# Second attention of a hybrid layer: scores, slot product and softmax two steps ahead of W2 instead of one

## The reference

```python
x = x + attn_a(layernorm(x))          # softmax attention, 16 heads of 128, (4, 256, 256) input
x = x + ffn(layernorm(x))             # int8-quantised 256x256 product
x = x + attn_b(layernorm(x))          # the attention of this document
x = x + ffn(layernorm(x))

def attn_b(hs):                       # per head: T = 256 positions, 128 features, M = 64 slots
    q, k = rope(hs @ Wq.T), rope(hs @ Wk.T);  v = hs @ Wv.T;  g = hs @ Wg.T
    s = clip(hs @ Ws1.T @ Ws2.T + bs2, -32, 32)
    es, enz = exp(s), exp(-cumlogsumexp(s, over positions))
    A  = tril(q @ k.T) * scale
    ok = enz * (A @ es);  qv = softmax(ok, over slots)
    W2 = tril((qv * enz) @ es.T)
    o  = W2 @ v
    o  = o * rsqrt(mean(o * o) + eps) * g_norm_weight * g * sigmoid(g)
    return o.reshape(T, H * 128) @ Wo.T
```

## Time and profile before

| | us |
|---|---|
| median of three runs (lowest, highest) | 821.48 (821.04, 825.55) |
| profiled execution, its own time | 821.59 |
| its span, first to last instruction | 819.7 |
| TensorE busy | 770.2 (94%) |
| VectorE busy | 581.3 (71%) |
| ScalarE busy | 435.4 (53%) |
| GpSimd busy | 285.7 (35%) |
| mean granted TensorE clock | 0.985 |

### The profile page before, as it was taken

How to read it: one execution, slowest core, us unless ns; L and a number is a source line. 1 busy time by engine, 2 the same in 40 slices (tenths; PEclk the granted TensorE clock), 3 DMA queues, 4 the chain that set the end, 5 groups by cost and what they waited for, 6 DMA issues and landing times.

```text
span 819.7 us, 14465 instructions
## 1 busy us (share of the span) xinstructions
PE 770.2 (94%) x4556; PEld 654.7 (80%) x4556; DVE 581.3 (71%) x1502; ACT 435.4 (53%) x1188; POOL 285.7 (35%) x291
## 2 busy tenths in 40 slices
PE   5899999999999995799999999999999999999963
PEld 4788888888888883478888888888888888888852
DVE  4555555555555558878887888798879888887686
ACT  3555565555556542465556465656564665555420
POOL 6311020201102014444536346355364463553222
PEclk9999999999999999899999999999999999999997
DMA  6110101101010100100101001001010010000001
...
DMA packets 23653, 23.74 MB, mean 29 GB/s; under 512 B 2369, under 2 KB 23361, under 8 KB 23506
## 3 DMA queue, kind: packets, MB, share of 16 engines
...
HBM read 22.45 MB, written 1.05 MB: 29 GB/s over the span
## 4 chain that ended last, share of the span: by engine, by line
PE 90%; DVE 5%; POOL 1%; ACT 1%; issue 1%; DMA 1%; SPq 0%; DVEq 0%; ACTq 0%; POOLq 0%
PE ps L1276 22%; PE ps L1483 11%; PE ps L1385 7%; PE ps L1283 5%; PE ps L1306 5%; PE ps L1349 3%; PE ps L1390 3%; PE ps L1495 3%; PE ps L1520 3%; PE ps L1325 3%; PE ps L1507 2%; PE ps L1402 2%; PE ps L1537 2%; PE ps L1539 2%; PE ps L1509 2%; PE ps L1508 2%
## 5 line engine op out<-in xcount | busy, mean ns | idle before, releaser
L1276 PE MATMUL ps<-xT_hi,w_hi 128*128 128x512 f32 x256 | 110.4, 431 | 5.3 <-DVE rot L1012 3.6
L1276 PE MATMUL ps<-xT_hi,w_lo 128*128 128x512 f32 x256 | 102.0, 399 | 0.0
L1276 PE MATMUL ps<-xT_lo,w_hi 128*128 128x512 f32 x256 | 101.5, 396 | 0.0
L1042 DVE TENSOR_TENSOR wt<-ps,const 128x384 f32<-128x384 f32 x128 | 68.2, 554 | 40.4 <-PE ps L1496 20.4
L383 POOL TENSOR_TENSOR w_lo<-w_raw,w_hi 128x512 fp32r<-128x512 f32 x32 | 40.8, 1285 | 155.8 <-ACT w_hi L535 154.1
L439 POOL TENSOR_TENSOR rot_s<-rot_s,const 128x512 f32<-128x512 f32 x64 | 82.1, 1293 | 21.1 <-ACT rot_s L678 21.1
L580 ACT ACTIVATE wt<-wt,negmax 128x128 f32<-128x128 f32 (+1 forms) x128 | 56.7, 444 | 28.2 <-DVE negmax L906 28.2
L894 DVE TENSOR_TENSOR v<-ps,bv_b 128x256 f32<-128x256 f32 x64 | 27.0, 422 | 51.9 <-PE ps L1283 51.9
L697 ACT ACTIVATE v<-ps 128x256 f32<-128x256 f32 x64 | 24.5, 382 | 72.4 <-PE ps L1483 72.2
L1276 PEld LDWEIGHTS ps<-xT_hi,w_hi 128*128 128x128 f32 x256 | 49.0, 192 | 15.1 <-issue 4.5
L1031 DVE RECIPROCAL enz<-zs 128x128 f32<-128x128 f32 x64 | 60.3, 943 | 1.0 <-ACT zs L684 1.0
...
## 6 DMA issues: line engine op xcount, KB each, us to landing
...
```

The lines of the kernel that those rows point to most:

```text
L1042: d.tensor_tensor(dst, src[:, 0:384], tri3, ALU.mult).then_inc(done, 1)
L1276: ins = mm(PJ[n[0]], w[:, m, c, h * P:(h + 1) * P], x[:, c, cols], start=(t == 0), stop=(t == len(terms) - 1))
```

## The change

One step more of lead, and everything is moved to fit:

- scores, slot scores, the exponential, its sum and the slot product are those of step x + 2 instead of x + 1; okeps has two halves, since two of them are now in use
- the transposes of qp and the copy zT are those of x + 1: they stand ahead of o, a whole step ahead of the W2 that reads them (`b_slot_transpose`, `b_z_copy`)
- projections move one step ahead: s to k1 stand in steps 1 and 3 of the step before, c0 to c3 in steps 0 and 2. `ti, tb` name the step that they used to stand in. So the prologue has the first s to k0 (k1 on TensorE) and the scores of step 1, and the last pair has projections in step 0 alone
- the order within a step is new on each engine; weight splits move from steps 1 and 2 to steps 0 and 1.

The core of the diff: the prologues of GpSimd and ScalarE, the new body and prologue of VectorE and TensorE. `...` marks what is left out; the lines taken out of a body stand in the functions above. ScalarE's and GpSimd's bodies change in the same manner.

```diff
@@ -506,6 +511,11 @@
...
+exp_tail(1, 1)
+rope_mul(slot_done(0, 1, B_TASKS.index("q0")), 0, 0)
+rope_mul(slot_done(0, 1, B_TASKS.index("q1")), 0, 1)
+rope_mul(slot_done(0, 1, B_TASKS.index("k0")), 1, 0)
+slots(1, 1)
...
@@ -794,8 +813,16 @@
...
+        s1_copy(3)
...
+b_task(0, 0, NB - 1, 0, 0)
+b_z_copy(0)
+b_task(0, 1, B_TASKS.index("s"), 1, 1)
+b_task(0, 1, B_TASKS.index("q0"), 1, 1)
+b_task(0, 1, B_TASKS.index("q1"), 1, 1)
+b_task(0, 1, B_TASKS.index("z"), 1, 1)
+b_task(0, 1, B_TASKS.index("k0"), 1, 1)
+b_okexp_step(1)
...
@@ -1068,100 +1095,105 @@
...
+def b_slots(x, k):
...
+    d.scalar_tensor_tensor(out=okeps[:, k, :], in0=oksum[:, :], scalar=RMS_EPS, in1=oksum[:, :],
...
+        ti, tb = (i, b + 1) if b < B - 1 else (i + 1, 0)
+        rest = not (last and b >= 1)
+        nxt = not (last and b >= 2)
+        half = 1 - tb // 2
+        phase = 2 * ti + 1 + tb // 2
...
+        def n(name):
+            j = B_TASKS.index(name)
+            return (*slot(ti, 1 + tb // 2, j), slot_ps(ti, 1 + tb // 2, j))
+        if b % 2 == 1:
+            if not (last and b == 3):
+                b_gate(slot(ti, tb // 2, NB - 1), phase - 1, 3, tb // 2)
+            if rest:
+                b_clip_s(n("s"), phase)
...
+            if last and b == 3:
+                ln_stats(3, 2, b_.y_acc, y_count(2))
+                ffn_out(1, 0)
+            if rest:
+                b_rope_cos(n("q0"), 0, 0)
+            if not (last and b == 3):
+                b_recip(None, tb // 2, 3)
+            if nxt:
+                b_scores(x + b + 2)
+            if rest:
+                b_rope_cos(n("q1"), 1, 0)
+            b_gated(x + b, b)
+            if rest:
+                b_recip(n("z"), half, 0)
+                b_rope_add(4 * phase + 1, 0, 0, half)
+            if nxt:
+                b_okn_max(x + b + 2, (b + 2) % B, 2 * i + (b + 2) // 2)
+            if not last:
+                out_tail(b_, x + b, b, O_)
+            if rest:
+                b_rope_cos(n("k0"), 0, 1)
+            if last and b == 3:
+                ffn_out(1, 1)
+                ln_scale(3, 2)
+                ffn_range(1, 2)
+            (add_y if last else add_group)(b_, x + b, b)
+            if rest:
+                b_rope_add(4 * phase + 2, 1, 0, half)
+            if nxt:
+                b_slots(x + b + 2, b % 2)
+        else:
+            if rest:
+                b_rope_add(4 * phase + 3, 0, 1, half)
+            for h in range(2):
+                b_mask(wt2[:, h, :], W_[h], b_w2_ps, 2 * (x + b) + h + 1, b_w2)
+            if rest:
+                b_rope_cos(n("k1"), 1, 1)
+                b_rope_add(4 * phase + 4, 1, 1, half)
...
+                b_gate(n("c0"), phase, 0, half)
+                b_recip(None, half, 1)
...
+                b_scores(x + b + 2)
+            b_gated(x + b, b)
+            if rest:
+                b_gate(n("c1"), phase, 1, half)
+                b_recip(None, half, 2)
+                b_gate(n("c2"), phase, 2, half)
+            if nxt:
+                b_okn_max(x + b + 2, (b + 2) % B, 2 * i + (b + 2) // 2)
...
+                b_slots(x + b + 2, b % 2)
...
+def n1(name):
+    j = B_TASKS.index(name)
+    return (*slot(0, 1, j), slot_ps(0, 1, j))
...
@@ -1198,8 +1230,20 @@
...
+b_slots(0, 0)
...
+b_gate(slot(0, 0, NB - 1), 0, 3, 0)
+b_clip_s(n1("s"), 1)
+b_rope_cos(n1("q0"), 0, 0)
+b_recip(None, 0, 3)
+b_scores(1)
+b_rope_cos(n1("q1"), 1, 0)
+b_recip(n1("z"), 1, 0)
+b_rope_add(5, 0, 0, 1)
+b_okn_max(1, 1, 0)
+b_rope_cos(n1("k0"), 0, 1)
+b_rope_add(6, 1, 0, 1)
+b_slots(1, 1)
...
@@ -1489,9 +1533,9 @@
...
-        if not (isinstance(x, int) and x == 0):
...
-            pe.wait_ge(b_w2, 2 * x + h - 1)
+        if not (isinstance(x, int) and x < 2):
...
+            pe.wait_ge(b_w2, 2 * x + h - 3)
...
@@ -1502,12 +1546,20 @@
...
+        pe.wait_ge(b_z, x)
...
+def b_slot_transpose(x):
...
+    pe.wait_ge(b_qp, x + 1)
+    for t in range(2):
+        ins = tr(X_qt[:, t * P:(t + 1) * P], qp[:, t, :], ident)
+    ins.then_inc(b_qt_ps, 1)
...
@@ -1543,72 +1595,34 @@
 def b_body(i, last):
     x = i * B
     for b in range(B):
...
+        ti, tb = (i, b + 1) if b < B - 1 else (i + 1, 0)
+        rest = not (last and b >= 1)
+        nxt = not (last and b >= 2)
+        half = 1 - tb // 2
+        phase = 2 * ti + 1 + tb // 2
+        c3_bank = slot(ti, 1 + tb // 2, NB - 1)[0]
+        if b % 2 == 1:
+            if rest:
+                b_task(ti, 1 + tb // 2, B_TASKS.index("s"), half, phase)
             b_w2_product(x, b, i)
...
             if last and b == 3:
                 ffn_product(1, 0)
                 ffn_transpose(1, 1)
+            if rest:
+                b_task(ti, 1 + tb // 2, B_TASKS.index("q0"), half, phase)
+            if not (last and b == B - 1):
+                b_slot_transpose(x + b + 1)
             b_o_product(x, b, i, last)
+            if rest:
+                b_task(ti, 1 + tb // 2, B_TASKS.index("q1"), half, phase)
             if nxt:
...
+                b_scores(x + b + 2, (b + 2) % B, 2 * i + (b + 2) // 2)
+            if rest:
+                b_task(ti, 1 + tb // 2, B_TASKS.index("z"), half, phase)
+                b_task(ti, 1 + tb // 2, B_TASKS.index("k0"), half, phase)
             if nxt:
...
+                b_ok(x + b + 2, (b + 2) % B, 2 * i + (b + 2) // 2)
             pe.wait_ge(b_og, x + b + 1)
             for h in range(2):
                 for t in range(2):
@@ -1618,9 +1632,7 @@
             if last and b == 3:
                 ffn_product(1, 1)
             if rest:
...
+                b_task(ti, 1 + tb // 2, B_TASKS.index("k1"), half, phase)
             if last:
                 pe.wait_ge(b_wos, PAIRS)
                 out_proj(b_, b, wos)
@@ -1628,7 +1640,44 @@
                 out_group(b_, i, b)
             if last and b == 3:
                 ffn_transpose(1, 2, (ffns[1].y, 1))
...
+        else:
+            b_w2_product(x, b, i)
+            if rest:
+                b_task(ti, 1 + tb // 2, B_TASKS.index("c0"), half, phase)
+            if last and b == 0:
+                out_group(b_, i, 0)
+            if rest:
+                b_task(ti, 1 + tb // 2, B_TASKS.index("c1"), half, phase)
+            if not (last and b == B - 1):
+                b_slot_transpose(x + b + 1)
+            b_o_product(x, b, i, last)
+            if nxt:
+                b_scores(x + b + 2, (b + 2) % B, 2 * i + (b + 2) // 2)
+            if rest:
+                b_task(ti, 1 + tb // 2, B_TASKS.index("c2"), half, phase)
+            if nxt:
+                b_ok(x + b + 2, (b + 2) % B, 2 * i + (b + 2) // 2)
+            pe.wait_ge(b_og, x + b + 1)
+            for h in range(2):
+                for t in range(2):
+                    o = (2 * h + t) * P
+                    ins = tr(O_[:, o:o + P], og[:, (2 * t + h) * P:(2 * t + h + 1) * P], ident)
+            ins.then_inc(b_ogt_ps, 1)
+            if rest:
+                b_task(ti, 1 + tb // 2, B_TASKS.index("et"), half, phase)
+            if last and b == 2:
+                for bank in range(2):
+                    pe.wait_ge(b_.proj_evac[bank], slot(PAIRS, 0, bank)[1])
+                ffn_transpose(1, 0)
+            if last:
+                pe.wait_ge(b_wos, PAIRS)
+                out_proj(b_, b, wos)
+            else:
+                out_group(b_, i, b)
+            if rest:
+                b_free(ti, 1 + tb // 2, NB - 1)
+                vg_chunk(c3_bank, 3, half, 0)
                 vg_chunk(c3_bank, 3, half, 1)
 pe.wait_ge(b_sums, 1)
@@ -1649,7 +1698,16 @@
         s1_product(2)
     if name == "et":
         s1_product(3)
+b_scores(1, 1, 0)
+b_slot_transpose(0)
+b_task(0, 1, B_TASKS.index("s"), 1, 1)
+b_task(0, 1, B_TASKS.index("q0"), 1, 1)
+b_task(0, 1, B_TASKS.index("q1"), 1, 1)
+b_ok(1, 1, 0)
+b_task(0, 1, B_TASKS.index("z"), 1, 1)
 pe.wait_ge(s1_done, 4)
+b_task(0, 1, B_TASKS.index("k0"), 1, 1)
+b_task(0, 1, B_TASKS.index("k1"), 1, 1)
 with pe.Fori(0, PAIRS - 1) as i:
     b_body(i, False)
 b_body(PAIRS - 1, True)
```

244 lines of the change are left out of this document (70 added, 174 removed).

## The result

The changed kernel takes 834.45 us (median of 4, 831.54 to 836.0) against 821.75 for the kernel before in the same session (4 runs, 821.04 to 825.55): ratio 1.0141, 95% interval 1.0097 to 1.0184. It is slower, as forecast, by 12.7 us (8 to 15 by the interval) and not by 6.6, and ends 0.45 us above the range. The profiled execution took 836.0 us, the longest of the four; its span is 834.2.

The account below looks back on a forecast made before the run. It took the loop as bound by TensorE and the tail by dependent chains. Loop -2.1, prologue stalls +3.5, clock +0.9 and tail +4.2 gave +6.5 on 821.59: 828.1 us, range 821.0 to 834.0.

Parts of the forecast that it names:

- What bounds the kernel: The loop is bound by TensorE, the tail by chains of dependent work; slower by more than 4.1 us had chance 0.63.
- Prologue, stall: Ahead of the loop, TensorE waits 2.8 us for the masks of scores(1), ready 8.3 us after c3's end.
- The 0.7 at the first o: End of the prologue: o could start at 17.5, its masks end near 18.2; a stall of 0.7 us.
- Prologue, clock: The prologue's long stall lowers the clock behind it; a stretch costs 1.7 us or nothing, taken as +0.9 us.
- Loop, gain: Loop: W2's waits for zT go, at most 0.3 us in two steps, 4.2 us in all; half taken, -2.1 us.
- rival 1: Loop: q1's rope add held behind GpSimd every odd-to-even turn; -2.1 becomes +1.4 to +5.6, 832 to 836 us; chance 0.2.
- Tail, chain: Last pair: three steps run as bare chains instead of two; 51.7 us against 48.1, +3.6 us.
- the bounds: Tail +4.2 us, bounds 0.5 (all idle of the new step filled) and 7 (a second stretch at lower clock).
- step 0's out projection: Last pair: it stands 0.8 us behind the first og transpose and needs 1.4; +0.6 us.
- the 5.1 us of work taken off: Tail: work still ahead of the last projection's end in the changed kernel, making 48.1 us the time to beat.
- Rivals 2 and 3: 2: loop gains 4.2, ends lose 2 each, 821.4 us, chance 0.25; 3: bare tail step free, 817 us, chance 0.07.

Follow-up runs that it names:

- e1: The changed kernel with VectorE making the masks of scores(1) right behind the clip in the prologue, ahead of cos(q0) and the reciprocal: 828.97 us, ratio 1.0091.
- b1: The kernel before with one edit: in even steps ScalarE copies zT before it evacuates c3 instead of behind it; 821.48 us, ratio 0.9986.

## Why the prediction was half right

- **What bounds the kernel, and that it gets slower:** held. By the sum of this document the ends cost, and the loop cannot pay them.
- **Prologue, stall:** held. Forecast 2.8, measured 3.08 idle (3.25 by e1); masks ready 8.3 us after c3's end, measured 8.3. The 0.7 at the first o was 0.33.
- **Prologue, clock:** the step that failed is the sentence that a stretch costs "1.7 us or nothing", of which I took 0.9. It cost 3.2 us in the changed kernel (e1), 3.1 to 3.3 in five more traces and 1.7 in two, never nothing. The 1.7 itself was no bad reading: in the kernel before, the rows behind the 3.60 us idle at 344.19 run at the lower level until 347.6, which loses as much. But it was taken as the most, and halved, while 4.9 us of dense work stood behind the idle, which at the lower level throughout would have lost 4.9.
- **Loop, gain:** mis-sized. The 0.25 us from s to W2 was read against a pitch that s does not have; b1 measures 0.06 and 0.15 in turn, 0.1 on average. In exchange the new order of c0, c1, z and k0 gives some 0.15 us in two steps that I had not seen (7 x 55.2 holds the 0.6 us wait of each pass and yet is only 0.65 longer than before). That it is the new order is inferred from what is left over, and which neighbours give it stays open.
- **Loop, rival 1:** its mechanism is real in all odd-to-even turns (1.04 us in place of 0.69), its price is not: it costs only in the turn at which VectorE's own loop adds 0.44 us, 7 x 0.6 = 4.2 us and not 14 x 0.4. Neither the forecast nor the rival had that turn. Result -2.1 forecast, +0.65 measured. That the time, 834.45, lies in rival 1's 832 to 836 is luck: its loop term of +1.4 to +5.6 did not come, and the clock at both ends made up for it, with the 1.5 us ahead of the changed code.
- **Tail, chain:** held to 0.7 us, but for the clock. From W2(1): o at 2.2 (forecast 2.4), og's transposes 7.6 (7.8), out projection 9.0 (9.2); W2(2) at 13.4 (11.7), and from there to the end 40.7 (40.0). Step 1 lost 1.7 us to the lower clock, which I had in the bounds only; where the clock stayed up (e1) it takes 11.75, what was forecast.
- **Sum:** 6.5 forecast; 13.0 without the 1.5 ahead of the changed code. The terms that differ: prologue +2.1 (clock +2.3, stall +0.45, first o -0.7, since its 0.33 lies in the loop), loop +2.75, tail +1.7 (step 1's clock; the rest of the tail agrees to 0.1 in sum: 0.7 more from W2(2) to the end, 0.3 less at step 0's out projection, where 0.6 was forecast and 0.30 measured, and some 0.4 less in the 5.1 us of work taken off). So of the 6.5 us missing the clock has 4.0 and the loop 2.75, with -0.2 for all else.
- **Rivals 2 and 3** fall: no end came out at half its count.

The Trainium skill (SBUF — State Buffer, "Who interferes with whom") says that a VectorE instruction with two SBUF inputs and a GpSimd instruction that reads SBUF exclude each other for a whole instruction, whoever comes first. The trace agrees, both ways. In the changed kernel, from the first W2 to the last turn at 766 us, all 15 rope adds that begin inside a GpSimd product end 0.53 to 0.55 us past its end, and none of the 42 others is held; GpSimd's product takes 1.48 us for 1.29 behind k0's add at 600.99. I had the rule and gave it 0.2.
